# Second attention layer: the gate's bias as a three-row bf16 product in place of a one-row fp32 product

## The reference, cut to what matters

```python
q = query @ Wq.T
gate = jax.nn.sigmoid(query @ Wg.T + bg)
k, v = jnp.split(kv @ Wkv.T, 2, axis=-1)
q, k = feature_map(q), feature_map(k)          # x > 0 ? x + 1 : exp(x), 16 heads of 16
kv_summary = jnp.einsum('bhsd,bhse->bhde', k, v)
z = 1.0 / (jnp.einsum('bhld,bhd->bhl', q, k.sum(axis=-2))[..., None] + EPS)
attn = jnp.einsum('bhld,bhde->bhle', q, kv_summary) * z
out = attn * gate @ Wo.T
x = x + jnp.tanh(g_xattn[1]) * out
```

## Time and profile before

| | |
|---|---|
| three runs, median (lowest, highest) | 1184.14 us (1183.31, 1185.34) |
| the profiled execution's own time | 1190.26 us |
| its span, first to last instruction | 1188.5 us |
| mean granted TensorE clock over the span | 0.883 |
| busy: PE, PEld, DVE, ACT, POOL | 919.3, 688.3, 790.6, 601.9, 481.0 us |
| the stage of the change | from 284 us to 420 us of the span |

### The profile page before, as it was taken

How to read it: one execution, slowest core, us unless ns; L and a number is a source line. 1 busy time by engine, 2 the same in 40 slices (tenths; PEclk the granted TensorE clock), 3 DMA queues, 4 the chain that set the end, 5 groups by cost and what they waited for, 6 DMA issues and landing times.

```text
span 1188.5 us, 20684 instructions
## 1 busy us (share of the span) xinstructions
PE 919.3 (77%) x5862; PEld 688.3 (58%) x5877; DVE 790.6 (67%) x2036; ACT 601.9 (51%) x1374; POOL 481.0 (40%) x555
## 2 busy tenths in 40 slices
PE   4737979974999966888778989986869999705386
PEld 3535879963777634444445655644658888604264
DVE  7846547856666667898567667653883455288885
ACT  3463237762444358799615566655214655303564
POOL 3277634545000012676343453422236777605200
PEclk9866989985999978899869999996979999955699
DMA  9834447756201010144360001002005333350001
GB/s 276 141 116 119 156 142 223 235 182 209 70 19 28 1 36 17 55 128 136 117 212 18 10 11 62 1 1 98 1 16 168 110 99 99 108 180 1 0 18 53
DMA packets 95965, 109.16 MB, mean 92 GB/s; under 512 B 14267, under 2 KB 85838, under 8 KB 95870
## 3 DMA queue, kind: packets, MB, share of 16 engines
q1 hardware_dynamic: 84158, 76.76, 22.3%
q0 software_dynamic: 11712, 31.20, 8.3%
HBM read 73.89 MB, written 34.03 MB: 91 GB/s over the span
## 4 chain that ended last, share of the span: by engine, by line
PE 47%; DVE 14%; ACT 8%; POOL 7%; issue 7%; DMA 4%; SPq 1%; ACTq 0%; DVEq 0%; POOLq 0%
PE bank L3137 7%; PE bank L3161 3%; PE bank L2694 3%; DVE resid L1010 3%; PE bank L1566 3%; POOL f_got L2050 2%; POOL f_outputs L2058 2%; PE bank L2735 2%; DMA f_back<-f_outputs 2%; PE bank L1592 2%; PE bank L2728 2%; PE bank L1854 2%; DVE ln_stat L222 1%; PE bank L1879 1%; PE bank L3496 1%
## 5 line engine op out<-in xcount | busy, mean ns | idle before, releaser
L3050 DVE TENSOR_TENSOR f_act<-f_silu,bank 128x256 f32<-128x256 f32 x54 | 22.8, 422 | 73.2 <-ACT f_silu L2973 71.8
L2468 POOL TENSOR_TENSOR work<-work 128x512 f32<-128x512 f32 x32 | 33.0, 1064 | 92.8 <-ACT work L2496 92.8
L2613 DVE TENSOR_REDUCE work<-bank 128x8 f32<-128x512 f32 x64 | 43.6, 682 | 34.9 <-PE bank L2694 34.6
L1271 POOL DMA_INDIRECT f_outputs<-f_y,f_places x39 | 41.4, 1062 | 56.8 <-ACT f_y L1332 34.9
L2920 POOL DMA_INDIRECT f_outputs<-f_y,f_places x54 | 54.6, 1012 | 23.8 <-issue 12.5
L2914 POOL DMA_INDIRECT f_got<-f_tokens,f_places x54 | 53.8, 996 | 22.7 <-issue 15.8
L599 POOL MEMSET f_scratch<- 128x64 f32 x2 | 0.3, 152 | 149.4 <-DVE resid L1789 133.5
L2050 POOL DMA_INDIRECT f_got<-f_tokens,f_places x39 | 38.2, 979 | 55.3 <-DVE f_places L956 37.8
L222 DVE BATCH_NORM_STATS2 ln_stat<-resid 128x6 f32<-128x256 f32 (+1 forms) x128 | 49.0, 414 | 4.1 <-DVE resid L2631 2.9
L1010 DVE SCALAR_TENSOR_TENSOR resid<-f_back,f_places,resid 128x256 f32<-128x256 f32 x80 | 36.4, 502 | 20.2 <-DMA f_back<-f_outputs 20.2
L2058 POOL DMA_INDIRECT f_outputs<-f_y,f_places x39 | 40.4, 1035 | 22.6 <-ACT f_y L2113 14.4
(11 more groups left out here) (534 smaller groups left out, 3253.4 us busy)
## 6 DMA issues: line engine op xcount, KB each, us to landing
f_back<-f_outputs SPq DMA_DIRECT2D x21, 256.0 KB, 4.6
f_back<-f_outputs SPq DMA_DIRECT2D x10, 512.0 KB, 6.3
f_got<-f_sorted SPq DMA_DIRECT2D x39, 129.0 KB, 2.9
f_sorted<-clear_row SPq DMA_DIRECT2D x1, 4992.0 KB, 27.6
raw<-in_L_ffn_w SPq DMA_DIRECT2D x24, 176.0 KB
tern_raw<-in_L_ffn_gate_w SPq DMA_DIRECT2D x8, 512.0 KB, 4.9
tern_raw<-in_L_ffn_up_w SPq DMA_DIRECT2D x8, 512.0 KB, 5.5
tern_raw<-in_L_ffn_down_w SPq DMA_DIRECT2D x8, 512.0 KB, 5.7
```

The source lines that it names most:

```text
L2613: dve.tensor_reduce(top[:, x % 2, :], got, AX.X, ALU.max).then_inc(s.top, 1)
```

## The change

The bias is loaded into three partitions instead of one. In front of step 0, VectorE splits it: part 0 is the bias rounded to bf16, part 1 the rest rounded to bf16, part 2 the rest of that. Multiplied by the columns of the identity and added up, they become three partitions of one bf16 tile, one part in each. The product then has three rows: weights of ones in bf16 (3 x 128), moving data 3 x 256 in bf16. PSUM adds in fp32, and the three parts of 8 significant bits each hold the fp32 value.

```diff
@@ layer1_attention
-            bias_row = ctx_sb[0:1, 0, :]
+            bias_rows = ctx_sb[0:3, 0, :]
+            bias_part, bias_rest = lay(3, D, dt=BF16)[0:3], lay(2, D)[0:3]
+            bias_parts, ones_b = lay(D, dt=BF16)[0:3], lay(P, dt=BF16)[0:3]
...
-                sp.dma_start(bias_row, io["L1_xattn_bg"].partition_broadcast(1)).then_inc(weight.loaded, 16)
+                sp.dma_start(bias_rows, io["L1_xattn_bg"].partition_broadcast(3)).then_inc(weight.loaded, 16)
...
+            def vector_bias(dve):
+
+                link = linker(dve, s.part)
+                dve.wait_ge(weight.loaded, was.loaded + 16 * 5)
+                dve.memset(ones_b, 1.0).then_inc(s.parts, 1)
+                left = bias_rows
+                for i in range(3):
+                    link(dve.tensor_copy(bias_part[:, i, :], left))
+                    if i < 2:
+                        link(dve.tensor_tensor(bias_rest[:, i, :], left, bias_part[:, i, :], ALU.subtract))
+                        left = bias_rest[:, i, :]
+                link(dve.tensor_scalar(bias_parts, bias_part[:, 0, :], ident[0:3, 0:1], None, ALU.mult))
+                link(dve.scalar_tensor_tensor(bias_parts, bias_part[:, 1, :], ident[0:3, 1:2], bias_parts, ALU.mult, ALU.add))
+                dve.scalar_tensor_tensor(bias_parts, bias_part[:, 2, :], ident[0:3, 2:3], bias_parts, ALU.mult, ALU.add).then_inc(s.parts, 1)
+
...
                 for t in range(2):
                     vector_norm(dve, t, t)
+                vector_bias(dve)
...
-                        pe.matmul(VAL[:, D:2 * D], ones[0:1, :], bias_row, start=False, stop=True).then_inc(s.val_ps, 1)
+                        if t == 0:
+                            pe.wait_ge(s.parts, 2)
+                        pe.matmul(VAL[:, D:2 * D], ones_b, bias_parts, start=False, stop=True).then_inc(s.val_ps, 1)
```

More of the change, by code:

```diff
@@ L1680, in layer1_attention @@
                 s.mask, s.ones, s.in_ps, s.inT, s.keyq_ps, s.val_ps, s.neg, s.grown, s.keyq, s.values,
-                s.gate, s.sum_ps, s.sum, s.num, s.den, s.att, s.attT_ps, s.attT, s.out
+                s.gate, s.sum_ps, s.sum, s.num, s.den, s.att, s.attT_ps, s.attT, s.out, s.part, s.parts
             ) = late.of("mask ones in_ps inT keyq_ps val_ps neg grown keyq values gate sum_ps sum num den att "
-                     "attT_ps attT out")
+                     "attT_ps attT out part parts")
             was = count_weights(loaded=16 * 5, turned=4, ready=DC * 4)
```

## The result

The changed kernel took 1177.06 us (median of 6 runs, 1174.91 to 1180.83), the kernel before 1185.30 (6 runs, 1183.31 to 1188.06) in the same measurement. The ratio is 0.994, with a 95% interval of 0.9923 to 0.9957: 7.1 us less by this ratio, between 5.1 and 9.1; the two medians by themselves are 8.2 apart. The forecast was 6.2 less.

The account below looks back on a forecast made before the run. TensorE was taken to bound the stage, with the bias product on its loop. 16 tiles x 0.39 us gave -6.2 us, all else nothing: 1184.14 to 1177.9 us, with a range of 1175.5 to 1181.5.

Parts of the forecast that it names:

- The bound: TensorE sets the stage of 16 tiles, with the bias product a link of its 8.00 us loop.
- The term per tile: Bias product in TensorE's loop: 0.30 us in place of 0.69, so 0.39 us less a tile.
- The upper bound, 0.42: Bias product: at most 0.69 - 0.27 = 0.42 us a tile goes, if its weight load costs nothing.
- The load in 107 ns by column count: Bias product: an uncovered weight load of 107 ns would leave 0.31 us gained a tile, 5.0 us in all.
- 16 tiles: The gain of 0.39 us reaches the loop in every one of 16 tiles: 6.2 us.
- The split: Nine VectorE instructions at the stage's head take 4.2 us (3.8 to 5.6), covered by 6.72 us of idle: no cost.
- The wider load: Loading the bias into three partitions puts two kilobytes more on SP's queue: no cost.
- One pass only: Rival at the bias product: only the second fp32 pass goes, 0.21 us a tile, 3.4 us, 1180.7 us; 9 in 100.
- No gain: Rival: the loop closes elsewhere, with VectorE the bound, and nothing comes of it, 1184.1 us; 6 in 100.
- A fall of the granted clock within the stage: Rival: TensorE's clock falls in the stage; two tiles at half clock give 1192 us; 3 in 100.
- f2_after's second theory: Expectation for the changed kernel's third run: 8 us or more gained, the part behind the stage over 2 us shorter.

Follow-up runs that it names:

- e1_again: The changed kernel run again without further change, on a slower chip: 1225.76 us, ratio 0.9949 to the kernel before.
- e2: The changed kernel with the bias product put back to one fp32 row, split and wider load kept: 1230.38 us, ratio 0.9996 to the kernel before.
- f1: The kernel before, unchanged, run and profiled again in the third set: 1184.23 us, ratio 1.0006.
- f2: The changed kernel a third time, in the third set: 1175.92 us, ratio 0.9934 to the kernel before.
- e6: The changed kernel with the five split instructions that make the parts run three times over: ratio 0.9960 to the kernel before.
- e5: The changed kernel with a bias product of 128 bf16 rows, 125 of them zero: ratio 0.9928 to the kernel before.
- e4: The changed kernel with the bias product and the bias left out, split kept: ratio 0.9922 to the kernel before.

## Why the prediction was right

**The bound** was read rightly: TensorE's loop set the stage, and what came off a link of the chain came off the period, 0.41 us in each of 14 periods and in tile 1.

**The term per tile** was 0.39 (0.69 less 0.30), and 0.41 came. The new MATMUL has 0.278 us, and its start isn't moved against its weight load at all: both stand at 343.36, so the 0.03 that I charged for the load isn't to be seen. I had taken the distance of two starts at L3496 for what the load costs; it isn't the load's length, which the record here gives as 90 ns. The upper bound, 0.42 for a load that costs nothing, was the better value. The load in 107 ns by column count isn't borne out as a price on the loop (5.0 us in all): 90 ns in the record, and none of it between the two starts. The 107 ns are an estimate from the Trainium skill (page "TensorE: Matmul & The Clock Gate", section "LDWEIGHTS (loading the stationary operand)"): the columns divided by 1.2. The row of L3496, a bf16 product of 256 columns at the same clock in another layer, was the right one to take.

**16 tiles** was not quite right, and two small misses cancel the 0.02. In tile 0 the gate isn't what L1866 waits for longest: the keys are. Their chain runs through a table load on ScalarE. In e1_again:

```profile
294.11 1.28 ACT L1757
295.40 0.01 issue
295.41 0.64 ACT work L1757
296.05 0.02 issue
296.07 0.70 DVE work L1826
296.77 0.44 issue
297.21 0.74 PE bank L1866 x8
```

From the end of L1826 to L1866 there are 0.44 us; before, from L1808's end (293.92) to L1848 (294.51 by the chain), 0.59, with the gate as the last. So tile 0 could give only some 0.15; the first L1866 comes 10.42 us after the first transpose, the first L1848 10.55, that is 0.13. I had compared the end of the keys with the end of the gate in a tile of the middle, where 0.84 us lie between them, and not in tile 0. And the last period lengthened, from 4.44 to 4.56; in it VectorE's scaling of the last tile is on the chain. 15 x 0.41 + 0.15 - 0.1 = 6.2, which is what the stage shows (136.4 - 130.2).

That it is 6.2 to the tenth is in part luck. With the same periods, the stage gives 7.3 from e2 to e1 and 5.5 from f1 to f2, since the granted clock's rise and fall move its two ends. In f1_before the clock rose 5.3 us after the first transpose, in the first profile of that kernel 8.0 us after it, and its first L1848 came at 9.81 us instead of 10.55. The changed kernel's first L1866 came at 10.42 in f2_after too (clock up at 7.2), so in that pair the clock's earlier rise took 0.6 us from the difference. And the last output projection took 2.06 us at 1.2 GHz in e2 and 1.12 at 2.4 GHz in e1. What all three pairs share is the 15 x 0.41 = 6.15 of the product, less 0.1 at the end.

**The split** cost nothing, as said: its cover was 6.72 us in the first profile and 6.12 in f1_before, where the clock rose early. It took 3.2 us, below my 3.8 to 5.6: the casts have 0.22 to 0.28 us, not the 0.41 I charged, and of the eight waits most show 0.04. **The wider load** had no effect on the stage's start.

**The rivals.** One pass only (0.21 a tile) is refuted by the period. No gain is refuted. A fall of the granted clock within the stage didn't come with the change: it stayed at 1.00 in the 13 periods,

```profile
299.68:398.35 98.67, 93.57 (x624) 74.43 (x624) 69.89 (x176) 43.75 (x104) 0.00 (x0) 1.00 0.11 34
```

with TensorE busy 95% of them, as worked out. It did come in e6, where TensorE's wait was long, and cost 1.6 us there.

**The rest of the measured gain.** By ratio the three measurements give 7.1, 6.3 and 7.8 us, each with an interval that holds 6.2. For the last two, 6 to 7 us were expected for the product alone and 8 or more if something else came with it; 6.3 lies in the first range, 7.8 between the two. In the slow chips' set the part behind the stage is equal with and without the fp32 product (809.9 and 810.1), which speaks against a gain there. On the faster chips the two profiles of the kernel before have 767 to 768 behind the stage, and the four of bf16 kernels 759 to 764, so what f2_after's second theory named, a part behind that is over 2 us shorter, did come there. Two against four profiles, with a spread of 5 us within the four, and 3.4 us among the slower chip's profiles, don't settle it; a gain of a microsecond or so outside the stage stays open. What the clock alone can do, the last output projection shows: 2.06 us in the first two profiles, 1.12 in e1_again.

## What to carry to other kernels

A product of few rows isn't cheap: the one fp32 row here took 0.62 us of the loop, and an fp32 product of 128 rows and the same columns 0.43 (L1899, two in 0.86). If the operand is a constant, its bf16 parts stacked in the rows of one product keep its value, and the price fell to 0.21. Price the piece by its link in the chain of waits, and check the first and last pass of a loop apart, since they wait for other things than the rest. A wait that covers new work has to be measured in more than one profile: with the same split it was 3.60 us in one profile and 2.95 in another, where the clock rose earlier. Once a small product sits between full ones, ask whether zero rows that keep the array's shape make it cheaper.

## What the runs showed of the hardware that I had not expected

- One bf16 product of 3 rows and of 1 row cost the loop the same 0.21 us; one of 128 rows, 125 of them zero, 0.11. PEld's 0.33 us of idle in front of it was there for one row of fp32 and for one and three of bf16, and gone with 128 rows of bf16 (e5).
- A wait of 2.58 us on TensorE inside a stage at 2.4 GHz was followed by a fall to 1.2 GHz that cost 1.6 us (e6). At the same place the wait of 1.12 us in the changed kernel, and those of up to 1.98 us (e4), were not.
- The first L1866 or L1848 came between 9.73 and 10.60 us after the stage's first transpose. It came at 9.73 to 9.81 where the clock rose 5.2 or 5.3 us after that transpose (e4, f4, f1) and at 10.41 or later where it rose after 7.2 us or more.
- Six profiles of kernels with the same code ahead of and behind the stage differ by up to 4.6 us ahead of it and 9.2 behind it. A difference of two spans says little of a change of 6 us; the period of the loop and the stage's own length, both read from one trace, repeat within 0.01 and 1.7 us for one kernel.
